# A deformable convolution block: third stage written out in full, second stage by pairs of tiles and begun in the first stage's last chunk

## The reference

```python
def _dcnv2(x, w_off, b_off, w, b, k, pad):
    om = lax.conv_general_dilated(x, w_off, (1, 1), [(pad, pad), (pad, pad)])
    om = om + b_off[None, :, None, None]
    oy, ox = (om[:, :P], om[:, P:2 * P])
    mask = jax.nn.sigmoid(om[:, 2 * P:])
    ...
    sy = oy + base_y[None]
    sx = ox + base_x[None]
    val = _bilinear(x, sy, sx) * mask[:, None]
    out = jnp.einsum('ncphw,ocp->nohw', val, w.reshape(w.shape[0], C, P))
    return out + b[None, :, None, None]
h = _bn_lrelu(_dcnv2(x, w_off1, b_off1, w1, b1, 1, 0), g1, bb1, m1, v1)
h = _bn_lrelu(_dcnv2(h, w_off2, b_off2, w2, b2, 3, 1), g2, bb2, m2, v2)
return x + h
```

## Time and profile before

| | us |
|---|---|
| median of 3 runs | 3175.01 |
| lowest and highest | 3172.33, 3175.93 |
| the profiled execution | 3181.72 |
| its span, first to last instruction | 3179.9 |

### The profile page before, as it was taken

One profiled execution on the slowest core, in us unless ns is written; L12 is line 12 of the kernel. 1 busy time (PEld: TensorE's weight loads), 2 busy tenths in 40 slices (PEclk: granted clock), 3 DMA queues, 4 the chain that ended last, 5 costly groups with the idle time before them and its releaser, 6 DMA issues.

```text
span 3179.9 us, 52201 instructions
## 1 busy us (share of the span) xinstructions
PE 3045.7 (96%) x15660; PEld 2472.5 (78%) x15660; DVE 2755.8 (87%) x4830; ACT 2510.6 (79%) x4736; POOL 1681.7 (53%) x1701
## 2 busy tenths in 40 slices
PE   6997888989999999999999999999999999999998
PEld 6997445558888888888888888888888888888888
DVE  5545899978999998998999998999989999999987
ACT  3665677778888888888888888888888888888886
POOL 0001444456656666566566666566666665666652
PEclk8999899989999999999999999999999999999999
DMA  8998999999999999999999999999999999999994
GB/s 310 322 339 299 352 349 332 334 332 398 373 357 378 368 362 376 365 365 379 359 370 377 357 372 374 356 381 367 359 379 363 364 368 350 362 362 352 367 347 174
DMA packets 432939, 1124.82 MB, mean 354 GB/s; under 512 B 42908, under 2 KB 173084, under 8 KB 432848
## 3 DMA queue, kind: packets, MB, share of 16 engines
q0 software_dynamic: 244672, 891.09, 75.1%
q1 hardware_dynamic: 116944, 161.19, 14.4%
q10 hardware_dynamic: 71232, 71.57, 6.5%
HBM read 1003.70 MB, written 137.04 MB: 359 GB/s over the span
## 4 chain that ended last, share of the span: by engine, by line
PE 69%; DVE 17%; issue 6%; ACT 5%; DMA 2%; ACTq 1%; DVEq 0%; SPq 0%; POOLq 0%
PE psum_t L1269 49%; PE psum_t L1256 9%; PE psum_t L386 5%; PE psum_t L697 4%; DVE arena L1190 4%; DVE val_first L1198 2%; DVE z_sb L1212 2%; DVE val_lo L1205 2%; DVE arena L835 1%; ACT val_hi L1153 1%; ACT psum_t L1139 1%; DMA arena<-w 1%; ACT z_sb L1162 1%; PE psum_t L682 1%; DVE arena L859 1%
## 5 line engine op out<-in xcount | busy, mean ns | idle before, releaser
L1125 POOL DMA_INDIRECT arena<-table,plan_in x1521 | 1516.2, 997 | 968.6 <-DVE arena L1198 419.0
L1269 PE MATMUL psum_t<-val_hi,w_hi 128*128 128x512 f32 (+2 forms) x3096 | 1240.4, 401 | 1.8 <-ACT z_sb L1162 0.5
L1269 PE MATMUL psum_t<-val_hi,w_lo 128*128 128x512 f32 (+2 forms) x3096 | 1200.2, 388 | 0.0
L1269 PE MATMUL psum_t<-val_lo,w_hi 128*128 128x512 f32 (+2 forms) x3096 | 1196.8, 387 | 0.0
L1139 ACT ACTIVATE psum_t<-arena,plan_in 128x512 f32<-128x512 f32 x1521 | 1044.1, 686 | 138.2 <-DVE arena L1190 133.9
L1190 DVE SCALAR_TENSOR_TENSOR arena<-arena,plan_in,psum_t 128x512 f32<-128x512 f32 x1521 | 1123.1, 738 | 10.6 <-ACT psum_t L1139 10.5
L1269 PEld LDWEIGHTS psum_t<-val_hi,w_hi 128*128 128x128 f32 x3096 | 582.6, 188 | 137.2 <-ACT z_sb L1162 36.2
L1269 PEld LDWEIGHTS psum_t<-val_hi,w_lo 128*128 128x128 f32 x3096 | 581.7, 188 | 121.1
L1205 DVE TENSOR_TENSOR val_lo<-psum_t,val_hi 128x1024 fp32r<-128x1024 f32 (+2 forms) x387 | 465.4, 1203 | 230.4 <-ACT val_hi L1153 230.3
L1269 PEld LDWEIGHTS psum_t<-val_lo,w_hi 128*128 128x128 f32 x3096 | 583.7, 189 | 102.9
L1153 ACT ACTIVATE val_hi<-psum_t 128x1024 fp32r<-128x1024 f32 (+2 forms) x387 | 390.0, 1008 | 281.2 <-PE psum_t L1256 281.0
(11 more groups left out here) (90 smaller groups left out, 2454.7 us busy)
## 6 DMA issues: line engine op xcount, KB each, us to landing
arena<-x SPq DMA_DIRECT2D x90, 512.0 KB, 8.3
table<-arena ACTq DMA_DIRECT2D x42, 896.0 KB, 8.3
out<-arena SPq DMA_DIRECT2D x136, 256.0 KB, 4.7
table<-arena ACTq DMA_DIRECT2D x42, 768.0 KB, 7.1
arena<-x SPq DMA_DIRECT2D x70, 384.0 KB, 6.3
arena<-table,plan_in POOLq DMA_INDIRECT x1521, 6.7
table<-table SPq DMA_DIRECT2D x32, 512.0 KB, 8.8
arena<-w POOLq DMA_DIRECT2D x2, 2304.0 KB, 13.9
```

The source lines that it names most:

```text
L1125: nc.gpsimd.indirect_dma_start(landing(r, i)[:, :], None, rows, bass.IndirectOffsetOnAxis(ap=row.bitcast(u32), axis=0))\
L1269: last = nc.tensor.matmul(psum_acc[:, oc, 0:n], a[:, w, oc * P:(oc + 1) * P], b[:, r % 2, kt, 0:n], start=(w == 0 and a is w2_hi and b is ...
```

## The change

- ACT, VectorE and TensorE: `position` is replaced by `in_full` in the third stage; each step is written out, with constants as wait values.
- Second stage: activate, the transposes and copy_h_t go by pairs of tiles (six pairs and a single tile a chunk), each pair with one instruction of VectorE and one of ACT. A pair is done when its second tile's turn comes; transposes of a pair fill one bank of PSUM.
- near(0) to near(3) and add_far(0) to add_far(2) stand in the last chunk of the first stage, one a tile, all through one bank of PSUM. plan(1) and its sigmoid move to t = 6 of the second stage. The last chunk's writes of table1 are issued by SP.
- The grid and its loads (13 of 117 KB) go. Tap offsets, less a half, are added to the bias of the offsets once; place adds pixel places by a broadcast and has six steps instead of seven.

```diff
+NEAR_AHEAD = 4
+FAR_AHEAD = 3
+PLAN_AT = 6
...
-        CHAIN = 7
+        CHAIN = 6
...
@@ first stage
+                for half, (j0, n) in enumerate(HALVES):
+                    sp.wait_ge(y_copied, (CHUNKS - 1) * CHUNK + 6 + j0 + n)
+                    table_writes(sp, table1, y_stage, CHUNKS - 1, half, table1_written[half])
...
+                pe.wait_ge(y_copied, TILES + 6)
...
                         if plans and j == 8:
                             modulation(0)
+                        if last and j >= CHUNK - NEAR_AHEAD:
+                            near(j - (CHUNK - NEAR_AHEAD))
...
-                chunk(CHUNKS - 1)
+                chunk(CHUNKS - 1, last=True)
                 for j in (CHUNK - 2, CHUNK - 1):
-                    copy_y(CHUNKS - 1, j)
-                modulation(1)
+                    copy_y(CHUNKS - 1, j, written=False)
+                return lambda: modulation(1)
...
+                        if last and j >= CHUNK - FAR_AHEAD:
+                            add_far(j - (CHUNK - FAR_AHEAD))
...
-                chunk(CHUNKS - 1)
-                plan(1)
+                chunk(CHUNKS - 1, last=True)
+                return lambda: plan(1)
...
@@ second stage
+            PAIRS = (CHUNK + 1) // 2
+            PAIR_AT = {c * CHUNK + min(2 * k + 1, CHUNK - 1): c * PAIRS + k
+                       for c in range(CHUNKS) for k in range(PAIRS)}
...
             def near_bank(t):
-                at = 512 * (5 + t % 2)
+
+                at = 512 * (6 if t < NEAR_AHEAD else 5 + t % 2)
...
-                    if c + 2 < CHUNKS:
-                        load_grid(c + 2)
...
+                def transpose_h(pair):
+                    c, j, n = pair_tiles(pair)
+                    pe.wait_ge(h_ready, tiles_to(pair))
+                    if pair >= 2:
+                        pe.wait_ge(h_t_ready, tiles_to(pair - 2))
+                    for i in range(n):
+                        for kt in range(KT2):
+                            last = nc.tensor.transpose(pair_bank(pair)[:, kt, i * P:(i + 1) * P],
+                                                       h_buf(c)[:, j + i, kt * P:(kt + 1) * P], ident[:, :])
+                    last.then_inc(h_transposed, n)
...
                 def near(t):
+                    if t == 0:
+                        act.wait_ge(y_copied, 6 + (CHUNKS - 1) * CHUNK + 7)
+                    if t == NEAR_AHEAD:
+                        act.wait_ge(y_copied, 6 + TILES)
+                    if t in (0, PLANNED):
+                        act.wait_ge(chain1, (1 + t // PLANNED) * PLAN_STEPS_1)
                     act.wait_ge(gathered[t % SLOTS], (t // SLOTS + 1) * 16)
-                    if t >= 2:
+                    if 1 <= t < NEAR_AHEAD:
+                        act.wait_ge(lines_ready, t)
+                    if t > NEAR_AHEAD:
                         act.wait_ge(lines_ready, t - 1)
...
+                def activate(pair):
+                    c, j, n = pair_tiles(pair)
+                    dve.wait_ge(sampled1, tiles_to(pair))
+                    v = h_buf(c)[:, j:j + n, :]
                     nc.vector.scalar_tensor_tensor(out=v, in0=v, scalar=SLOPE, in1=v,
-                                                   op0=ALU.mult, op1=ALU.max).then_inc(h_ready, 1)
+                                                   op0=ALU.mult, op1=ALU.max).then_inc(h_ready, n)
...
-                    link(nc.vector.tensor_scalar(k, s, 0.0, float(HEIGHT - 1), ALU.max, ALU.min), at + 2)
-                    link(nc.vector.tensor_scalar(k, k, -0.5, ROUND, ALU.add, ALU.add), at + 3)
-                    link(nc.vector.tensor_scalar(k, k, ROUND, None, ALU.subtract), at + 4)
-                    link(nc.vector.tensor_tensor(s, s, k, ALU.subtract), at + 5)
...
+                    link(nc.vector.tensor_scalar(k, s, -0.5, HEIGHT - 1.5, ALU.max, ALU.min), at + 2)
+                    link(nc.vector.tensor_scalar(k, k, ROUND, ROUND, ALU.add, ALU.subtract), at + 3)
+                    link(nc.vector.tensor_tensor(s, s, k, ALU.subtract), at + 4)
...
-                act.wait_ge(const_ready, 1)
-                act.wait_ge(chain1, 2 * PLAN_STEPS_1)
-                near(0)
...
+                        if NEAR_AHEAD <= t + 1 < TILES:
+                            near(t + 1)
+                        if t - 2 in PAIR_AT:
+                            copy_h_t(PAIR_AT[t - 2])
+                        if t == PLAN_AT - 1:
+                            late_modulation()
...
+                        if t == PLAN_AT:
+                            late_plan()
+                        if FAR_AHEAD <= t < TILES:
+                            add_far(t)
...
+                        if t - 1 in PAIR_AT:
+                            activate(PAIR_AT[t - 1])
...
@@ third stage
+            def in_full(step, after=0, first=0):
+
+                for r in range(first, ALL_TAPS + after):
+                    step(0, r)
...
-                return begin_unit, lambda: upper(0, 0), lambda: position(act, step, after=5, first=2)
+                return begin_unit, lambda: upper(0, 0), lambda: in_full(step, after=5, first=2)
...
-                return begin_units, lambda: position(dve, step, after=5, first=2)
+                return begin_units, lambda: in_full(step, after=5, first=2)
...
-                return lambda: transpose(0, 0), lambda: position(pe, step, after=1, first=1)
+                return lambda: transpose(0, 0), lambda: in_full(step, after=1, first=1)
```

More of the change, by code:

```diff
@@ L423, in modulation, with chunk @@
                         .then_inc(gate_ready, 1)
-                def chunk(c, first=False, plans=False):
+                def chunk(c, first=False, plans=False, last=False):
                     for j in range(CHUNK):
@@ L429, in chunk @@
                         if j >= 2:
-                            copy_y(c, j - 2)
+                            copy_y(c, j - 2, written=not last)
                         elif not first:
@@ L519, in plan, with chunk @@
                     assert steps[0] == PLAN_STEPS_1, steps
-                def chunk(c, first=False, plans=False, slabs=()):
+                def chunk(c, first=False, plans=False, last=False, slabs=()):
                     slabs = list(slabs)
@@ L826, in on_scalar, with run @@
-                begin_upper()
-                modulation(CHUNKS - 1)
-                hats(CHUNKS - 1)
+                def run(late_modulation):
+                    act.wait_ge(const_ready, 1)
+                    for t in range(TILES + DRAIN):
+                        if NEAR_AHEAD <= t + 1 < TILES:
[4 more added lines that the diff above has]
+                            late_modulation()
+                        for dy in range(3):
+                            if t - 7 - dy in BAND_AT:
+                                fold_band(BAND_AT[t - 7 - dy], dy)
+                        c, j = divmod(t, CHUNK)
+                        if 1 <= c < CHUNKS:
+                            if j == 9:
+                                keep_tail(c - 1)
+                            if j == 10:
+                                modulation(c - 1)
+                            if j == 12:
+                                hats(c - 1)
+                        for half, (j0, n) in enumerate(HALVES):
+                            end = t - 1 - (j0 + n)
+                            if end >= 0 and end % CHUNK == 0 and end // CHUNK < CHUNKS:
+                                act.wait_ge(h_ready, end + j0 + n)
+                                table_writes(act, table2, h_buf(end // CHUNK), end // CHUNK, half,
+                                             table2_written[end // CHUNK % 2][half], copies_of(end // CHUNK))
+                        if 0 <= t - TILES - 1 < BEGUN:
+                            if t == TILES + 1:
+                                act.wait_ge(lines_ready, TILES)
+                                act.wait_ge(upper_added, TILES)
+                            begin_unit(t - TILES - 1)
+                    begin_upper()
+                    modulation(CHUNKS - 1)
+                    hats(CHUNKS - 1)
@@ L830, in on_vector @@
+                return near, run
             def on_vector(dve, begin_units):
-                dve.wait_ge(bias_ready, 1)
                 def add_far(t):
@@ L1331 @@
     a = {k.removeprefix("L0_conv_"): np.asarray(v) for k, v in inputs.items()}
-    where, grid = pixel_constants()
+    where, tap_at = pixel_constants()
     arrays = {
@@ L1346 @@
         "where": where,
-        "grid": grid,
+        "tap_at": tap_at,
         "identity": np.eye(P, dtype=np.float32),
```

175 lines of the change are left out of this document (71 added, 104 removed).

## The result

The changed kernel takes 3151.9 us, the median of four runs (3150.6 to 3154.9), against 3174.8 us for the kernel before beside it (3172.3 to 3175.9): 0.993 of it, 95% interval 0.9913 to 0.9948, 22.9 us less. The prediction was 3163 us, with a range of 3148 to 3173. The time lies in the range, but at rival B's 3151 and not at the sum's.

What follows compares the result with a forecast made beforehand. TensorE was taken to set the third stage's pace, VectorE and TensorE the second's. Third stage 1.7, seam 3.4, second stage 6.6 and hand-over 0.3 sum to 12.0 us off the 3175.0 median: 3163 us, range 3148 to 3173.

Steps and rivals of the forecast that it cites:

- rival B: Second stage: TensorE's clock no longer falls, ten chunks save 1.8 us and one 0.73; 3151 us, chance 0.28.
- the sum: Whole kernel: 1.7 + 3.4 + 6.6 + 0.3 = 12.0 us saved, 3163 us; likeliest case, chance 0.47.
- The clock: Second stage: four of eleven chunks without TensorE's clock fall, three more than now; 6.6 us saved, between 0 and 20.
- Pairs and link: Second stage, VectorE: paired activates save 0.41 us and one link less in place 0.32, 0.73 us a chunk.
- The seam: First to second stage: add_far(3) 7.1 us earlier, less 3.7 for the moved plan(1); net 3.4 us, range 1 to 5.5.
- The loop of ACT and VectorE: Seam: upper, lower, add_far and near wait on each other, 2.8 us a tile for three tiles; 1.3 us charged.
- The third stage in full: Third stage: writing out the loop saves 0.045 us a group over 38 groups, 1.7 us, bounds 0 and 3.4.
- rival F: Third stage: each branch back stalls for a fetch, hidden alike in both halves; 103 us less, 3072 us, chance 0.01.
- C: Second stage gains eaten by TensorE's stretch, seam down to 1 us; 3 us saved, 3172 us, chance 0.16.
- D: Second stage: TensorE's clock falls twice a chunk as it waits for pairs; slower, 3185 us, chance 0.06.
- E: Third stage: instruction pages come late, 72 pages with 1 us each; 3247 us, chance 0.02.
- The hand-over: Second to third stage: the last place has one link less on the path, 0.3 us saved.

Runs made afterwards that it cites:

- before, filled: Kernel before with twelve unused TensorE products of 128x256 ahead of the transposes of tile 11 of each chunk from the second on: 3461.3 us, 0.997 of the kernel before.
- old start: Changed kernel with both modulations and plans ahead of the second stage again and nothing of it in the first stage's last chunk: 3150.0 us, 0.9912 of the kernel before.
- single tiles: Changed kernel with its second stage by single tiles instead of pairs: 3159.0 us, 0.9944 of the kernel before.
- six links alone: Kernel before with one edit, place in six links through a grid shifted by a half: 3264.6 us, 1.028 of the kernel before.
- filled hand-over: Changed kernel with 32 unread TensorE products of 128x512 between the second stage and the wait for the third's first samples: 3149.5 us, 0.9927 of the kernel before.
- seven links: Changed kernel with rounding in place written as two instructions again: 3166.7 us, 0.9964 of the kernel before.
- the first set: First four follow-up kernels run together: kernel before again, with idle filled, with third stage in full, and changed kernel with loops; there the kernel before took 3468 us.
- The loop at its old place: Changed kernel with third stage as loops and one first-stage memset split in 25, so VectorE's loop starts at instruction 1225: 3149.1 us, 0.9923 of the kernel before.

## Why the prediction was right in its range and wrong in its likeliest case

**The clock, the step that failed.** The terms for a chunk were right: 27.1 us with the fall and 25.45 without were forecast, 27.09 and 25.44 measured. The number of chunks was not: I took four of eleven without the fall, and there were ten. It hangs on the idle time at place, which I put at "about 2.0 us". The terms I named there give less: 2.22, less 0.32 for the link, less 0.1 to 0.2 for TensorE's work ahead of it, is 1.7 to 1.8. Measured: 1.78; 1.90 with the link alone, and 0.12 for the pairs. So the forecast was in its range because rival B had set the lower end, and its likeliest case was wrong. The right sum alone would not have given ten chunks either: the rows before show no idle at place between 1.8 and 2.2 us, so where in between the clock stops falling was a guess. A smaller slip: the sum gives 0.15 us to the chunk that had no fall before, where by its own terms it gets 0.73.

How the fall hangs on the idle time, over all fourteen traces, ten chunks each (from the second on, without the last, shorter one):

| idle at place | kernels | chunks with the fall behind it |
|---|---|---|
| 0.8 to 1.1 us | before, filled | 0 of 10 |
| 1.77 or 1.78 us | changed (two traces) and five traces of its variants, old start among them | 0 of 61 |
| 1.90 us | single tiles; six links alone | 1 of 10; 3 of 10 |
| 1.93 or 1.95 us | changed, its loops, filled hand-over | 3 of 5 |
| 2.08 or 2.09 us | seven links; changed with loops | 9 of 10 |
| 2.22 us | before (two traces), before with the third stage in full | 22 of 28 |

The six chunks that are left had 0.4 to 1.4 us (four, no fall), 2.40 (none) and 2.47 us (a fall). Length alone does not decide: 1.90, 1.95, 2.08 and 2.22 us went both ways, 2.22 us not more often than 2.09, and all five chunks of 1.93 or 1.95 us are the third of their kernel. But between 1.78 and 2.09 us, a link of place, the falls go from none to nearly all.

**Pairs and link.** 0.73 us a chunk forecast; 0.63 measured, 0.32 of it the link (26.07 to 25.75, exact) and 0.31 the pairs.

**The seam.** 3.4 us forecast; about 1.9 by the traces, with a spread of 3, inside the 1 to 5.5. The loop of ACT and VectorE was right (2.73 us a tile for 2.8; 297.63 to 300.36 above), add_far(3) came 4.1 us behind the start of the last lower for 5.3 forecast, and plan(1) takes its 3.9 us among the tiles. The mis-sized term is ACT's DMA issue of 2.49 us, which I credited in full, though ACT goes from it into a wait. Its copy of the last chunk's tile 6 waits until the same tiles of the chunk before have been written from that buffer. ACT issues that write in both kernels, and the change does not touch it. In the kernel before:

```profile
281.14 1.04 ACTq L294 DMA_DIRECT2D table<-arena  x2
...
295.84 0.38 ACT L411 ACTIVATE arena<-psum_t 128x256 f32<-128x256 f32 x1 [2.46 <-DMA table<-arena]
```

From that issue to the end of the wait are 14.7 us before and 13.4 after (279.07 to 292.45). With the 2.49 us of issue gone from in between (0.97 to 2.49 in the six traces with the old start), ACT only waits longer, 3.85 us instead of 2.46. Most of the spread of the seam is this transfer's: with 13.1 to 13.4 us for it the new start takes 25.5 to 26.1 us by the measure above, with 15.4 to 16.0 us 27.7 to 28.7; the old start takes 27.5, 29.0 and 29.9 us with 13.2, 14.0 and 14.7. In the first set ACT does not wait there at all, and the same distance is 26.4 us in the three traces with the old start and 23.3 in the one with the new, 3.1 us less. So the sum was near for a seam without the wait.

**The third stage in full.** 1.7 us forecast for 38 groups, 1.75 by the first two traces. The loop at its old place against the code in full says 58.58 against 58.54 to 58.57 us a group, 0.4 to 1.5 us in all, and the medians show none of it (3149.1 and 3151.5). But its worth within this change is another: the rest of the change moves VectorE's loop from instruction 1225 to 1201, and there loops cost 34 us, more than all else gained, 1.0035 instead of 0.993. The prediction missed this. It weighed the branch as a property of branching ("the equal halves speak against"); the halves were equal because the loop happened to lie well. Stops once a pass, as rival F had them, do exist, with some five more instruction packets each; they were only not there in the kernel before.

**The other rivals.** C (3172) and D (3185, two falls a chunk) did not come: all through the chunk from 482 to 510 us of the changed kernel the granted clock is 1.00, and TensorE's next longest idle there is 0.86 us. E did not come either: 85 instruction packets on q8 and 89 on q14 from 812 to 3000 us, with TensorE busy 98.7%. **The hand-over** gave 0.3 us from the last place to TensorE's first tap (8.09 to 7.77), as forecast.

The sum of what was found, in time of the profiled executions: 18.1 for the chunks (ten without the fall instead of one), 3.6 at the last place and behind it, and 8.9 up to the first place, of which some 1.9 are the seam by the later traces; the first stage of the first trace of before was among the latest, and its execution 6.9 us above its median.

## What to carry to other kernels

Where an engine's clock falls behind an idle time, work out that idle time to the tenth of a microsecond, since there a small saving on the engine it waits for can be worth several times its own length (a link of 0.31 us, 3.4 in eleven chunks, was worth 11 to 12). Before counting on a loop, or on its removal, find out how long its body is on each engine and where it starts: an edit in another stage can move it and cost 1 to 3%. Before crediting an engine with an instruction or a DMA issue taken off it, look at what it waits for next: a wait that ends at its own time takes the saving back.

## What the hardware showed that was not expected

- A loop of 297 instructions on VectorE (counted in the program, like its places) ran without a stop from its instruction 1225, and stopped in each pass from 1213 (4.0 and 2.8 us, 5.7 a pass in the end) and from 1201 (4.7 us, 2.0 a pass).
- The same kernel had the lower clock in ten of eleven chunks in one execution and in six in another.
- On one chip the kernel before took 3468 us in one set of runs and 3176.6 in another. From 700 to 3450 us of the first, TensorE was busy 91%, DMA moved 325 GB/s where the earlier trace rows have 361. Why is open, and so is why code in full gained 1% there:

```profile
700.00:3450.00 2750.00, 2514.05 (x12122) 2039.83 (x12122) 2226.19 (x3715) 2042.18 (x3547) 1485.30 (x1489) 0.98 0.90 325
```
